# An attention and mixture-of-experts kernel: the entry of its expert loop reordered, the spline tile's last block split off, and the output copy on two queues

## What is computed

```python
x = x + attn(layernorm(x))      # 16 heads: causal linear attention on 2nd-order features, and a 64-wide window
x = x + ffn(layernorm(x))
# ffn: every row goes to its best 2 of 8 experts, weighted
w_full = one_hot(top_k(softmax(x @ gate_W), 2)) * normalized weights
mlp_out = gelu(x @ mlp_W1[e] + b1) @ mlp_W2[e] + b2                    # experts 0..3, 128 -> 512 -> 128
z       = rswaf(layernorm(x), grid) @ kan_sl_W0[e] + b0                # experts 4..7 ("spline"), 128*8 -> 256
kan_out = rswaf(layernorm(z), grid) @ kan_sl_W1[e] + b1                # 256*8 -> 128
out = sum over experts of w_full * expert_out
# rswaf(x, grid) = 1 - tanh((x - grid)/2)**2, for 8 grid points
```

## Time and profile before

| | us |
|---|---|
| median of 3 runs | 814.43 (813.74 to 817.10) |
| the profiled execution | 813.58 |
| its span, first to last instruction | 811.8 |
| PE busy | 727.2 (90%) |
| ACT busy | 531.6 (65%) |
| POOL busy | 494.7 (61%) |
| DVE busy | 474.2 (58%) |
| first weighting of an MLP tile | 454.69 to 456.09 |
| last matmul | 785.3 |
| output copy issued, landed | 803.05, 811.4 |

### The profile page before, as it was taken

How to read it: one execution, slowest core, us unless ns; L and a number is a source line. 1 busy time by engine, 2 the same in 40 slices (tenths; PEclk the granted TensorE clock), 3 DMA queues, 4 the chain that set the end, 5 groups by cost and what they waited for, 6 DMA issues and landing times.

```text
span 811.8 us, 20472 instructions
## 1 busy us (share of the span) xinstructions
PE 727.2 (90%) x7113; PEld 556.6 (69%) x7114; DVE 474.2 (58%) x1116; ACT 531.6 (65%) x697; POOL 494.7 (61%) x699
## 2 busy tenths in 40 slices
PE   5499999999999999999989699999999999999860
PEld 2246566575656656566567599989988989899760
DVE  6732655646475554665446594956976949775510
ACT  3577687777767778686783475775876757782700
POOL 9432656465575656657567578668777577656341
PEclk9799999999999999999999799999999999999985
DMA  2530220403114040221361444364463553633124
GB/s 40 160 99 16 72 82 2 142 13 107 48 40 114 3 138 16 85 68 42 91 188 49 97 141 138 69 161 97 131 167 95 127 151 57 164 87 28 14 22 118
DMA packets 72959, 70.61 MB, mean 87 GB/s; under 512 B 20866, under 2 KB 65186, under 8 KB 70948
## 3 DMA queue, kind: packets, MB, share of 16 engines
q1 hardware_dynamic: 55444, 56.88, 22.9%
q0 software_dynamic: 16912, 11.35, 9.8%
q10 hardware_dynamic: 480, 0.79, 0.3%
HBM read 49.43 MB, written 21.37 MB: 87 GB/s over the span
## 4 chain that ended last, share of the span: by engine, by line
PE 69%; DVE 10%; ACT 7%; POOL 5%; issue 4%; DMA 2%; DVEq 0%; ACTq 0%; SPq 0%; POOLq 0%
PE pv L1556 16%; PE ring L1523 13%; PE pv L1643 11%; PE ring L1602 6%; PE ring L1615 4%; PE ring L1490 4%; PE ring L1507 3%; ACT Pb L934 3%; DVE maxima L1192 3%; PE ring L1583 2%; DVE h L1244 2%; PE ring L1705 2%; PE ring L1443 1%; DVE lo L1048 1%; PE ring L1544 1%
## 5 line engine op out<-in xcount | busy, mean ns | idle before, releaser
L934 ACT ACTIVATE Pb<-ring 128x1024 f32<-128x1024 f32 x160 | 156.5, 1025 | 60.8 <-PE ring L1602 58.8
L746 POOL DMA_INDIRECT acc_d<-stack,recs x84 | 138.2, 1645 | 61.7 <-issue 33.3
L767 POOL TENSOR_SCALAR_AFFINE_SELECT Pb<-Pb 128x512 f32<-128x512 f32 x128 | 78.9, 637 | 131.3 <-ACT Pb L934 131.3
L1125 DVE SCALAR_TENSOR_TENSOR stack<-stack 128x512 f32<-128x512 f32 x160 | 103.0, 688 | 59.4 <-ACT stack L912 57.0
L1523 PE MATMUL ring<-stack 128*128 128x256 f32 x560 | 124.0, 381 | 2.5 <-issue 2.3
L1643 PE MATMUL pv<-Pb,vaug 128*32 128x192 f32 (+4 forms) x2048 | 120.4, 376 | 2.3 <-POOL Pb L767 1.6
L1523 PEld LDWEIGHTS ring<-stack 128*128 128x128 f32 x560 | 105.4, 190 | 19.8 <-issue 5.5
L912 ACT ACTIVATE stack<-ring,kprm 128x512 f32<-128x512 f32 x160 | 108.2, 814 | 0.1
L1602 PE MATMUL ring<-stack 128*128 128x128 f16 (+3 forms) x512 | 90.5, 306 | 17.5 <-DMA stack<-hl_d 10.1
L943 ACT ACTIVATE Pb<-ring 128x768 f32<-128x768 f32 (+1 forms) x128 | 88.2, 760 | 15.6 <-PE ring L1615 12.9
L1643 PEld LDWEIGHTS pv<-Pb,vaug 128*32 128x32 f32 x2048 | 60.0, 109 | 55.9 <-issue 37.5
(11 more groups left out here) (237 smaller groups left out, 1148.4 us busy)
## 6 DMA issues: line engine op xcount, KB each, us to landing
stack<-L_ffn_kan_sl_W SPq DMA_DIRECT2D x20, 1024.0 KB, 5.2
stack<-hl_d SPq DMA_DIRECT2D x23, 256.0 KB
stack<-L_ffn_mlp_W SPq DMA_DIRECT2D x12, 256.0 KB
stack<-hl_d SPq DMA_DIRECT2D x23, 128.0 KB
hl_d<-hi SPq DMA_DIRECT2D x7, 384.0 KB, 2.6
hl_d<-lo SPq DMA_DIRECT2D x7, 384.0 KB, 3.3
Pb<-L_ffn_mlp_W SPq DMA_DIRECT2D x10, 256.0 KB, 5.4
xb<-L_attn_x SPq DMA_DIRECT2D x9, 256.0 KB, 2.8
```

The lines of the kernel that those rows point to most:

```text
L746: pool.indirect_dma_start(acc_d, bass.IndirectOffsetOnAxis(ap=recs[:, kind, u % RECS, q, 0:1], axis=0), src[:, u % 2, q, :], None, compute ...
L934: act.activation(Pb[:, n % 2, at:at + 1024].rearrange("p (k q) -> p k q", k=2), slot(job), ACT.Square, bias=1.0).then_inc(freed[job % SLOT ...
L1125: dve.scalar_tensor_tensor(basis[z][g], s_, -1.0, s_, ALU.add, ALU.mult).then_inc(k_bas[z], 1)
```

## The change

- **Ahead of the loop**, DVE's order is now: statistics of spline tile 0, the copy for MLP tile 1, the weighting of MLP tile 0, four basis functions of spline tile 1, the norm of spline tile 0, the other four, and then the counts.
- **The spline tile's last block.** PE multiplies the blocks in the order 3, 2, 1, 0. Block 0 goes to the first bank of the middle ring slot, the one that `hidden_transposed` writes for the next tile; that function therefore waits for `k_y` of the tile before. A new semaphore `k_three` says that blocks 1 to 3 are multiplied. DVE weights these three by two operations (`k_three_y`) and block 0 by two more (`k_y`). POOL scatters blocks 1 to 3 behind `k_three_y` and block 0 behind `k_y`.
- **The copy.** POOL raises `all_added` with each landed tile. SP, behind its own loop, runs a loop of 24 passes that raises it once for every tile that there is not, so that the waits are for the constant 49. SP copies one half of the output and ACT the other, and SP waits for both.
- The bias of an MLP tile is added by a `tensor_tensor` in place of a `scalar_tensor_tensor` with factor 1.

```diff
+        k_three, k_three_y = sem("k_three"), sem("k_three_y")
+        def copy_half(eng, m):
+            eng.wait_ge(all_added, 2 * TURNS * UNROLL + 1)
+            eng.dma_start(out[B // 2 * m:B // 2 * (m + 1)].rearrange("b t d -> (b t) d"),
+                          acc_d[TS + B * T // 2 * m:TS + B * T // 2 * (m + 1)]).then_inc(copied, 16)
...
-            sp.wait_ge(all_added, 1)
-            sp.dma_start(out.rearrange("b t d -> (b t) d"), acc_d[TS:]).then_inc(copied, 16)
-            sp.wait_ge(copied, 16)
+            with sp.Fori(0, TURNS * UNROLL) as k:
+                with sp.If(k >= n_kind[1]):
+                    sp.sem_inc(all_added, 1)
+                with sp.If(k + 1 >= n_kind[0]):
+                    sp.sem_inc(all_added, 1)
+            copy_half(sp, 0)
+            sp.wait_ge(copied, 32)
...
+                if kind == 1:
+                    for ready, blocks in ((k_three_y, range(1, Q4)), (k_y, (0,))):
+                        pool.wait_ge(ready, tile_no(k))
+                        pool.sem_inc(pool_at, 1)
+                        for q in blocks:
+                            scatter_block(1, u, q)
...
                 pool.sem_inc(added, 1)
+                pool.sem_inc(all_added, 1)
...
-            pool.sem_inc(all_added, 1)
...
+            copy_half(act, 1)
...
+            def weighted_blocks(i, u):
+                k = i * UNROLL + u
+                dve.wait_ge(k_rec[u % RECS], use_no(RECS, i, u, 16))
+                dve.wait_ge(k_w1[u % 2], use_no(2, i, u, 32))
+                dve.wait_ge(k_added, tile_no(k, back=2))
+                for m, (y, at, n, products, parts) in enumerate((
+                        (pv[:, 1, P:], 1, Q4 - 1, k_three, k_three_y), (ring[:, 1, 0, 0:P], 0, 1, k_mm[1], k_y))):
+                    shape = [P, n, D]
+                    part = k_res[:, u % 2, at:at + n]
+                    dve.wait_ge(products, tile_no(k))
+                    dve.scalar_tensor_tensor(part, y.rearrange("p (q d) -> p q d", d=D), -4.0,
+                                             k_bias1[u % 2].unsqueeze(1).to_broadcast(shape), ALU.mult, ALU.add
+                                             ).then_inc(w_sum[1], 1)
+                    dve.wait_ge(w_sum[1], tile_no(k, 2, m + 1))
+                    dve.tensor_tensor(part, part, weight[:, 1, u % RECS, at:at + n, 1:2].to_broadcast(shape),
+                                      ALU.mult).then_inc(parts, 1)
...
-            n_kind = load_counts(dve)
-            basis_functions(0, 0, 1)
             hidden_stats(0, 0)
             copy_rows(0, 1)
-            weighted(0, 0, 0)
+            weighted(0, 0)
+            basis_functions(0, 0, 1, range(G // 2))
             hidden_norm(0, 0)
+            basis_functions(0, 0, 1, range(G // 2, G))
+
+            n_kind = load_counts(dve)
...
                 pe.wait_ge(k_sig[1], tile_no(k, 2 * G, back=1))
+                pe.wait_ge(k_y, tile_no(k, back=1))
...
-                        mm = pe.matmul(pv[:, 1, P * q:P * (q + 1)], basis[1][g][:, P * q:P * (q + 1)],
+                        mm = pe.matmul(pv[:, 1, P * q:P * (q + 1)] if q else ring[:, 1, 0, 0:P],
+                                       basis[1][g][:, P * q:P * (q + 1)],
...
-                for_blocks(blocks, products, k_mm[1])
+                with pe.If(blocks > 3):
+                    products(3)
+                with pe.If(blocks > 2):
+                    products(2)
+                products(1).then_inc(k_three, 1)
+                products(0).then_inc(k_mm[1], 1)
```

More of the change, by code:

```diff
@@ L737, in gather, with scatter_block @@
                         ap=recs[:, kind, u % RECS, q, 0:1], axis=0)).then_inc(x_sem[u % n], 16)
+            def scatter_block(kind, u, q):
+                src, add_sem = ((m_res, m_add), (k_res, k_add))[kind]
+                pool.indirect_dma_start(acc_d, bass.IndirectOffsetOnAxis(ap=recs[:, kind, u % RECS, q, 0:1], axis=0),
+                                        src[:, u % 2, q, :], None, compute_op=ALU.add).then_inc(add_sem, 16)
             def scatter_add(kind, i, u):
-                y_sem, add_sem, added, src = ((m_y, m_add, m_added, m_res), (k_y, k_add, k_added, k_res))[kind]
                 k = i * UNROLL + u
-                pool.wait_ge(y_sem, tile_no(k))
-                pool.sem_inc(pool_at, 1)
-                for q in range(Q4):
-                    pool.indirect_dma_start(acc_d, bass.IndirectOffsetOnAxis(ap=recs[:, kind, u % RECS, q, 0:1], axis=0),
-                                            src[:, u % 2, q, :], None, compute_op=ALU.add).then_inc(add_sem, 16)
+                if kind == 0:
+                    pool.wait_ge(m_y, tile_no(k))
+                    pool.sem_inc(pool_at, 1)
+                    for q in range(Q4):
+                        scatter_block(0, u, q)
+                if kind == 1:
+                    for ready, blocks in ((k_three_y, range(1, Q4)), (k_y, (0,))):
+                        pool.wait_ge(ready, tile_no(k))
+                        pool.sem_inc(pool_at, 1)
+                        for q in blocks:
+                            scatter_block(1, u, q)
             def end_of_add(kind, i, u):
@@ L1097, in copy_rows, with weighted @@
                 dve.tensor_copy(mxs, m_banks[0]).then_inc(m_xs, 1)
-            def weighted(kind, i, u):
+            def weighted(i, u):
                 k = i * UNROLL + u
-                rec_sem, added, mm_sem, dst, y_sem, y, bias, bias_sem = (
-                    (m_rec, m_added, m_mm, m_res, m_y, m_banks[1], m_bias, m_w2),
-                    (k_rec, k_added, k_mm[1], k_res, k_y, pv[:, 1, :], k_bias1, k_w1))[kind]
-                dve.wait_ge(rec_sem[u % RECS], use_no(RECS, i, u, 16))
-                dve.wait_ge(bias_sem[u % 2], use_no(2, i, u, 32))
-                dve.wait_ge(added, tile_no(k, back=2))
-                dve.wait_ge(mm_sem, tile_no(k))
-                full = [P, Q4, D]
-                dve.scalar_tensor_tensor(dst[:, u % 2], y.rearrange("p (q d) -> p q d", d=D), (1.0, -4.0)[kind],
-                                         bias[u % 2].unsqueeze(1).to_broadcast(full), ALU.mult, ALU.add
-                                         ).then_inc(w_sum[kind], 1)
-                dve.wait_ge(w_sum[kind], tile_no(k))
-                dve.tensor_tensor(dst[:, u % 2], dst[:, u % 2], weight[:, kind, u % RECS, :, 1:2].to_broadcast(full),
-                                  ALU.mult).then_inc(y_sem, 1)
@@ new lines, in weighted @@
+                dve.wait_ge(m_rec[u % RECS], use_no(RECS, i, u, 16))
+                dve.wait_ge(m_w2[u % 2], use_no(2, i, u, 32))
+                dve.wait_ge(m_added, tile_no(k, back=2))
+                dve.wait_ge(m_mm, tile_no(k))
+                full = [P, Q4, D]
+                dve.tensor_tensor(m_res[:, u % 2], m_banks[1].rearrange("p (q d) -> p q d", d=D),
+                                  m_bias[u % 2].unsqueeze(1).to_broadcast(full), ALU.add).then_inc(w_sum[0], 1)
+                dve.wait_ge(w_sum[0], tile_no(k))
@@ new lines, in weighted @@
+                dve.tensor_tensor(m_res[:, u % 2], m_res[:, u % 2], weight[:, 0, u % RECS, :, 1:2].to_broadcast(full),
+                                  ALU.mult).then_inc(m_y, 1)
+            def weighted_blocks(i, u):
[14 more added lines that the diff above has]
+                                      ALU.mult).then_inc(parts, 1)
@@ L1396, in _ @@
                         with dve.If(k + 1 < n_kind[0]):
-                            weighted(0, i, u + 1)
+                            weighted(i, u + 1)
                         with dve.If(k + 2 < n_kind[1]):
@@ L1402, in _ @@
                         with dve.If(k < n_kind[1]):
-                            weighted(1, i, u)
+                            weighted_blocks(i, u)
         @blk.tensor
@@ L1453, in _ @@
             pe.wait_ge(wout_loaded, 32)
-            tile_lead(pe, (m_xT, 1), (m_h, F // P), (m_mm, 1), (k_xT, 1), (k_hT, 1), (k_mm[0], 1), (k_mm[1], 1))
+            tile_lead(pe, (m_xT, 1), (m_h, F // P), (m_mm, 1), (k_xT, 1), (k_hT, 1), (k_mm[0], 1), (k_mm[1], 1), (k_three, 1))
             def rows_transposed(kind, i, u):
```

2 lines of the change are left out of this document (1 added, 1 removed).

## The result

The changed kernel takes **822.27 us** (median of 6 runs, 820.88 to 822.86) where the kernel before takes 814.15 in the same series: ratio 1.0091, 95% interval 1.0076 to 1.0107. It is slower by 8 us; forecast were 808.9 us, and 802.5 to 812.3 as the range. The profiled execution took 822.4 us, its span is 820.3.

What follows compares the result with a forecast made beforehand. PE bounds the kernel (69% of the chain of waits), with waits at loop entry, last spline tile and behind PE. Terms -2.5 + 3.1 - 5.3 = -4.7 us took 813.58 to 808.9 us, range 802.5 to 812.3.

Steps and rivals of the forecast that it cites:

- The walk: Tail: POOL's branches over skipped passes, from the last landing to its closing DRAIN, were forecast to stay at 6.5 us.
- the tail's -5.3: After the loop: earlier scatters and copy, with POOL's closing DRAIN then last, end the span 5.3 us earlier.
- Entry, -2.5: Loop entry: DVE's new order starts PE's long products earlier, 4.9 us at full clock, 2.5 with a clock fall.
- rival C: Loop entry: the clock stays at 1.0, 2.4 us less, 806.5 us; chance 0.15.
- the 461.5 that was named as a sign of being wrong: Loop entry: PE starting later than 461.5 would show the forecast wrong; its long products were expected at 459 to 461.
- Loop, +3.1: Expert loop: PE's transposes wait for DVE's weighting behind two short spline tiles, 1.6 and about 1.5 us, 3.1 us slower.
- The price of 0.56 and 0.29 us per operation: Loop: a DVE weighting operation takes 0.56 us for three blocks and 0.29 for one.
- Tail, first half: After the loop: POOL's first spline scatter starts at 784.3, not 787.51; last landing at 793.4, where the copy starts.
- Rival B: Tail: POOL's closing DRAIN isn't a fixed length, PE's walk ends the span: 3.3 us less, 805.6; chance 0.20.
- Rival D: Loop: the new waits of 1.6 us let the clock fall, 6.9 us in all: 815.8, no change; chance 0.10.
- Rival E: Tail: SP's counting loop of 24 passes isn't done in time, delaying the copy: about 834 us; chance 0.05.

Runs made afterwards that it cites:

- the copy behind the walk: Changed kernel, with both halves of the output copy started only after POOL's branches over skipped passes: 917.8 us against 910.4 for the kernel before, ratio 1.0092.
- the three instructions more: Changed kernel, with three repeated, already met waits ahead of POOL's loop: 904.7 us against 900.6 for the kernel before, ratio 1.0042.
- the early copy alone: Kernel before, with only SP's counted wait and one 2 MB copy issued at the last landing: 915.1 us against 910.4, ratio 1.0078.

## Why the prediction was wrong, step by step

It forecast a span of 807.1; it is 820.3, 13.2 us more. The walk makes 10.8 of them (17.3 - 6.5), the late start of the loop, behind the fall of the clock at 419, makes 1.56, and the last landing 0.9, as it came 9.0 us behind the last matmul and not 8.1. Entry and loop together came out within 0.1 us of their terms.

- **The step that failed**, as the prediction put it: "But POOL still walks its 6.5 us after 793.4", with "what two queues do to the copy costs or gives nothing while POOL is last". It took the walk for a constant and moved it, with everything behind it, over to a time when the copy runs. The row was there: 3.4 us at one jump, in which q14 moved two packets of instructions, is a fetch, and a fetch is a DMA; the same edit put 2 MB of DMA under it (5.4 us by the corners of the table) and one semaphore instruction ahead of the loop (5.3 us). With 17.3 in the place of 6.5 the tail's -5.3 becomes +5.5. The landing's 0.9 brings that near the measured +6.2 (32.8 after, 26.5 before). That both causes are true at once, and add up, is shown by the copy behind the walk and by the three instructions more.
- **Entry, -2.5**: right: 2.3 us in the two traces, 2.1 and 2.7 by the means of all. The clock fell, as the value taken assumed. The first GELU came at 457.7, with 1.56 us of the late start in it: 456.1, as worked out. So rival C did not come. PE's long products began at 461.99, past the 461.5 that was named as a sign of being wrong; without the late start it is 460.4.
- **Loop, +3.1**: right in mechanism and nearly in size. 1.57 and 1.32 us of wait at the two transposes named, 0.87 at a third tile; from tile 1's transposes to those of the last tile PE lost 3.7, and 0.7 of it came back behind them. The price of 0.56 and 0.29 us per operation held. The experiments also show the loop's spread: in seven of the nine profiles with the split it took 289.8 to 292.9 us, and in the two others POOL's coefficients came some 4 us late, PE waited 5.3 us at one tile, the clock fell there, and the loop took 296 to 297.5 us. None of the five profiles without the split shows that (286.2 to 287.2). Why in those two only is open.
- **Tail, first half: right in mechanism, 0.9 us too short.** First spline scatter 0.75 us behind its semaphore step, the copy issued 0.12 us behind the last landing. That landing is at 796.5 and not near 794: 2.3 us of it are PE's later end, which the loop and the clock moved. The rest is that the MLP tile's landing, which POOL must see first, came 3.4 us later than before (786.7 against 783.3).
- **Rival B** (no fixed DRAIN): false here. 6.28 us in every profile but the last, where it was 6.85. The Trainium skill ("VectorE: DVE Perf Modes", section "The DRAIN you can't avoid") says about 12 ns, on all five engines, of the DRAINs that the runtime puts ahead of and behind a program. Those here carry a line of the kernel: PE's 8 ns agree with that figure and POOL's 6.28 us don't.
- **Rival D** (815.8): not in the changed kernel's two profiles; waits of 1.6 us left the clock at 1.00 there. It is what happened in the two others, at a wait of 5.3.
- **Rival E** (SP late) is false: a pass takes 0.7 us. It had the right sign, by a far jump on the wrong engine. Its own argument, that a far jump costs 3.4 us, was the one to ask of POOL.

The prediction cited the Trainium skill, "Runtime: NRT & Kernel Launch", section "Instruction fetch mechanics", against rival E. The same section says that an engine holds two pages of instructions, fetched in order, and that a branch out of them waits for a DMA. By that rule a loop's head that lies across the border of two pages needs both of them, and drops the one with the loop's end, to which the next branch goes: three fetches instead of one. The traces agree: one instruction ahead of the loop makes two more stalls of 2.1 to 3.3 us and three more packets on q14, four make none. Where the border lies no view shows.

## What to carry to other kernels

The end of a program is code too: where an engine leaves a loop by branches over skipped bodies, its time is that of fetches, and they wait when a bulk transfer is started under them. Start the last copy when no engine that could end last has a far jump left to make, or let such an engine make it before the data are ready. A price read from one branch holds for the layout and the traffic of that trace: one instruction ahead of a loop was worth 5 us here.

## What the runs showed of the hardware

- Bulk DMA delays the fetch of instructions. The last q14 packet of POOL's far jump starts 1.0 to 1.1 us behind the jump in the four traces in which the copy is issued behind the walk, 5.2 to 5.8 us in the five with the 2 MB copy under it in packets of 64 KB, and 4.2 us with packets of 4 KB. PE's first q8 packet starts 0.6 to 0.8 us behind its far jump without the copy, which then takes 4.8 to 5.2 us, and 3.5 to 3.9 us behind it where the copy was issued 3 us or more before, which makes it 7.8 to 8.1. Where the copy was issued only 0.3 to 0.5 us before, the jump took 6.7 us in two runs and 4.7 in the early copy alone.
- Two halves of a copy on two queues land no sooner than one DMA: 7.7 and 8.5 us against 8.4 and 8.6 with no far jump beside them, 7.7 to 7.9 and 10.9 to 11.2 against 8.9 to 11.0 with one. They are issued together, but q10's first data packet starts 3 us behind q1's (801.1 and 798.0 in the changed kernel). The Trainium skill, "DMA: Bandwidth & Descriptors", section "Issuing engines are not separate DMA queues", says that DMAs of all engines run on the same 16; the traces agree.
- The clock fell at 419 in both profiled executions of the changed kernel and in none of three others of the 814 us series, behind an idle stretch of PE that all of them have. From the transposes at 417 to 418 to the first-layer products it took 28.5 and 28.7 us with the fall and 27.0 to 27.1 without, so the fall costs 1.4 to 1.7 us. Its cause is open.
